# Weights loaded in two parts, a shorter routing in other steps, and high parts copied by ScalarE

## What is computed

```python
# attention: 16 heads of 8, causal
q, k, v = split(xn @ in_proj.T)
attention = softmax(q @ k.T / sqrt(8) + mask) @ v @ out_proj.T
# ffn: one shared expert and the best 2 of 7 routed ones, inner size 352
logits = xn @ wr.T + rb
probs = softmax(logits)
scores, idx = top_k(probs, 2)
scores = scores / scores.sum()
w = sum(scores * one_hot(idx, 7))
def expert(x, g, u, d): return (silu(x @ g.T) * (x @ u.T)) @ d.T
ffn = expert(xn, sg, su, sd) + sum(w[e] * expert(xn, rg[e], ru[e], rd[e]) for e in range(7))
```

## Time and profile before

| | |
|---|---|
| time, median of 3 | 493.08 us (491.39 to 498.99) |
| the profiled execution | 494.13 us |
| its span | 492.4 us |
| busy TensorE, VectorE, ScalarE, GpSimd | 442.4, 378.0, 300.3, 292.8 us |
| mean granted TensorE clock | 0.994 |

### The profile page before, as it was taken

One profiled execution on the slowest core, in us unless ns is written; L12 is line 12 of the kernel. 1 busy time (PEld: TensorE's weight loads), 2 busy tenths in 40 slices (PEclk: granted clock), 3 DMA queues, 4 the chain that ended last, 5 costly groups with the idle time before them and its releaser, 6 DMA issues.

```text
span 492.4 us, 12367 instructions
## 1 busy us (share of the span) xinstructions
PE 442.4 (90%) x3981; PEld 326.1 (66%) x3985; DVE 378.0 (77%) x915; ACT 300.3 (61%) x633; POOL 292.8 (59%) x415
## 2 busy tenths in 40 slices
PE   8988888888989999999888999989979999989995
PEld 4766555555556666666565788766867777868884
DVE  6996999899987888888774477565754888756886
ACT  2536666666767676766767666455554765655652
POOL 1446977778778888888788301643626585565200
PEclk9999999999999999999999999999989999999998
DMA  9885899889765565666364226676747577641762
GB/s 253 246 263 171 300 327 306 270 293 298 249 224 153 157 173 163 184 163 179 107 238 172 82 82 222 212 252 233 259 149 272 204 249 253 240 147 34 243 200 66
DMA packets 53215, 102.00 MB, mean 207 GB/s; under 512 B 10245, under 2 KB 28426, under 8 KB 48928
## 3 DMA queue, kind: packets, MB, share of 16 engines
q1 hardware_dynamic: 48672, 92.73, 58.5%
q0 software_dynamic: 4480, 8.47, 5.1%
HBM read 62.49 MB, written 39.46 MB: 207 GB/s over the span
## 4 chain that ended last, share of the span: by engine, by line
PE 49%; issue 6%; ACT 5%; DMA 4%; POOL 4%; DVE 3%; another core or an unknown queue 1%; SPq 0%; DVEq 0%; ACTq 0%; POOLq 0%
PE ps L801 10%; PE ps L803 9%; PE ps L802 9%; PE ps L867 4%; PE ps L928 4%; PE ps L875 3%; DMA sb_wb<-wd 3%; ACT sb_work L671 3%; POOL xs L582 2%; PE ps L1091 2%; PE ps L948 2%; POOL sb_work L606 2%; PE ps L931 2%; DVE sb_v_all L1396 1%
## 5 line engine op out<-in xcount | busy, mean ns | idle before, releaser
L671 ACT ACTIVATE sb_work<-ps 128x768 f32<-128x768 f32 x128 | 104.4, 815 | 68.8 <-PE ps L863 67.5
L1287 DVE TENSOR_REDUCE sb_blockmax<-ps 128x6 f32<-128x768 f32 x128 | 122.3, 957 | 23.8 <-PE ps L875 17.6
L627 POOL DMA_INDIRECT ys<-sb_v_all,sb_xn_all x76 | 78.6, 1035 | 93.1 <-DVE sb_v_all L1417 73.1
L606 POOL TENSOR_SCALAR_AFFINE_SELECT sb_work<-sb_work 128x512 f32<-128x512 f32 x128 | 82.5, 646 | 32.0 <-ACT sb_work L671 28.9
L802 PE MATMUL ps<-sb_ring,sb_wb 128*128 128x512 f32 (+1 forms) x231 | 83.5, 362 | 0.0
L1396 DVE TENSOR_TENSOR sb_v_all<-ps,sb_v_all 128x512 f32<-128x512 f32 (+1 forms) x93 | 57.4, 617 | 21.4 <-PE ps L803 8.0
L582 POOL DMA_INDIRECT xs<-sb_xn_all,sb_posu x64 | 62.6, 978 | 10.7 <-issue 10.7
L867 PE MATMUL ps<-sb_ring 32*128 32x256 f32 x256 | 49.2, 375 | 14.7 <-ACT sb_work L671 9.5
L751 ACT ACTIVATE sb_v_all<-ps 128x512 f32<-128x512 f32 (+1 forms) x93 | 49.6, 533 | 15.5 <-PE ps L803 12.6
L801 PE MATMUL ps<-sb_ring,sb_wb 128*128 128x512 f32 (+1 forms) x138 | 52.0, 377 | 5.4 <-issue 2.8
L867 PEld LDWEIGHTS ps<-sb_ring 32*128 32x128 f32 x256 | 25.2, 181 | 38.1 <-issue 35.3
(11 more groups left out here) (172 smaller groups left out, 1075.4 us busy)
## 6 DMA issues: line engine op xcount, KB each, us to landing
sb_wb<-wd SPq DMA_DIRECT2D x25, 1152.0 KB, 5.7
sb_ring<-qk SPq DMA_DIRECT2D x64, 256.0 KB
wd<-sb_wb SPq DMA_DIRECT2D x8, 1152.0 KB, 5.8
xs<-sb_o_all SPq DMA_DIRECT2D x19, 260.0 KB, 3.6
qk<-sb_ring SPq DMA_DIRECT2D x32, 128.0 KB
sb_work<-ys SPq DMA_DIRECT2D x16, 256.0 KB, 3.3
sb_xn_all<-xs SPq DMA_DIRECT2D x15, 260.0 KB, 3.8
sb_o_all<-w SPq DMA_DIRECT2D x8, 384.0 KB, 3.5
```

The lines of the kernel that those rows point to most:

```text
L606: pool.affine_select(out=o, in_=o, compare_op=ALU.is_ge, fill=0.0, base=0, pattern=[[0, 4], [1, 128]], channel_multiplier=-1)\
L627: pool.indirect_dma_start(out=ys_d, out_offset=bass.IndirectOffsetOnAxis(ap=row, axis=0), in_=yst[i % NYS][:, EMB * j:EMB * j + EMB], in_o ...
L671: act.activation(part.rearrange("p (k h q) -> p h k q", h=2, q=128), ps[:, 4:6, 0:HEAD].rearrange("p h (k q) -> p h k q", q=128), ACT.Exp, ...
L1287: dve.tensor_reduce(blockmax[:, a:b + 1, 0:3], ps[:, a:b + 1, 0:HEAD].rearrange("p h (k c) -> p h k c", c=128), AX.X, ALU.max).then_inc(s[ ...
```

## The change

**Weights' loads.** In `wb` and `wd` the columns are ordered by gate, up and down first and by third second, and not the other way round. `load_weights` is replaced by `load_gate_up`, which waits for the last use of gate and up of the buffer (semaphores U and G), and `load_down`, which waits for the last down product (dn) as before. Each has semaphores of its own. In SyncE's loop the order is now gate and up, tokens, down.

**Routing.** The exponentials are not divided by their sum, since the division cancels in the normalised weights of the two chosen experts; the first choice is found from b, which is zero at the maximum; the weight of the first expert is 1 / (1 + e). The two choices stand in bfloat16 and are counted by two matmuls each instead of being added first. The running sum is shifted by one place, so that the ends needn't be copied. It has 19 parts instead of 25, in the steps that N_ROUTE lists, and the counts are in steps 7 and 11.

**High parts.** The copy of L563 moves from GpSimd to ScalarE (`high_block`), behind the first of a step's two exponentials; the very first stands in the front. GpSimd's low part is made in the same steps as before.

```diff
-        N_COUNT = (11, 15)
-        N_ROUTE = 25
+        N_COUNT = (7, 11)
+        N_ROUTE = (0, 1, 2, 3, 5, 6, 7, 9, 10, 11, 13, 14, 15, 17, 18, 19, 21, 29, 33)
...
+        def block_parts(e, k):
+            to = [wb[e % 3][:, WC * h:WC * h + WC].rearrange("p (m t c) -> p m t c", t=MT, m=3)[:, :, k, :]
+                  for h in range(2)]
+            return stage[e % 2][:, WB * k:WB * k + WB].rearrange("p (m c) -> p m c", m=3), *to
...
-            def load_weights(w):
-                if w > NR + 1:
-                    return
+            def load_rows(w):
+                if 1 <= w <= NR:
+                    e = sp.value_load(etab[0:1, w - 1:w], min_val=0, max_val=ROUTED - 1)
+                    return wd[bass.ds(e * 128, 128), :].rearrange("p (h c) -> p h c", h=2)
+                return wd[ROUTED * 128:EXPERTS * 128, :].rearrange("p (h c) -> p h c", h=2)
+            def load_gate_up(w, rows):
+                if w >= 3:
+                    sp.wait_ge(s["U"], MT * (w - 3 + EARLY))
+                    sp.wait_ge(s["G"], MT * (w - 3 + EARLY))
+                to = wb[w % 3][:, :].bitcast(F32).rearrange("p (h c) -> p h c", h=2)
+                sp.dma_start(to[:, :, 0:2 * WB], rows[:, :, 0:2 * WB]).then_inc(s_wgu[w % 3], 16)
+            def load_down(w, rows):
                 if w >= 3:
                     sp.wait_ge(s["dn"], MT * (w - 3 + EARLY))
-                if 1 <= w <= NR:
-                    e = sp.value_load(etab[0:1, w - 1:w], min_val=0, max_val=ROUTED - 1)
-                    rows = wd[bass.ds(e * 128, 128), :]
-                else:
-                    rows = wd[ROUTED * 128:EXPERTS * 128, :]
-                sp.dma_start(wb[w % 3][:, :].bitcast(F32), rows).then_inc(s_wb[w % 3], 16)
+                to = wb[w % 3][:, :].bitcast(F32).rearrange("p (h c) -> p h c", h=2)
+                sp.dma_start(to[:, :, 2 * WB:WC], rows[:, :, 2 * WB:WC]).then_inc(s_wdn[w % 3], 16)
...
             for r in range(NR):
+                if r + 3 <= NR + 1:
+                    rows = load_rows(r + 3)
+                    load_gate_up(r + 3, rows)
                 load_tokens(r + 3)
-                load_weights(r + 3)
+                if r + 3 <= NR + 1:
+                    load_down(r + 3, rows)
...
-            def split_block(e, k):
-                part, low = slice(WB * k, WB * k + WB), slice(WC + WB * k, WC + WB * k + WB)
-                if k == 0:
-                    pool.wait_ge(s_wld[e % 2], LOADED[e])
-                    if e >= 3:
-                        pool.wait_ge(s_wd[e % 3], 16 * (e // 3))
-                pool.tensor_copy(wb[e % 3][:, part], stage[e % 2][:, part]).then_inc(s["wcp"], 1)
+            def low_block(e, k):
+                parts, high, low = block_parts(e, k)
                 pool.wait_ge(s["wcp"], MT * e + k + 1)
-                for c in range(0, WB, 128):
-                    a, z = part.start + c, low.start + c
-                    last = pool.tensor_tensor(wb[e % 3][:, z:z + 128], stage[e % 2][:, a:a + 128],
-                                              wb[e % 3][:, a:a + 128].bitcast(F32), ALU.subtract)
+                for m in range(3):
+                    last = pool.tensor_tensor(low[:, m, :], parts[:, m, :], high[:, m, :].bitcast(F32), ALU.subtract)
                 last.then_inc(s["wlo"], 1)
...
+            def high_block(e, k):
+                if k == 0:
+                    act.wait_ge(s_wld[e % 2], LOADED[e])
+                    if e >= 3:
+                        act.wait_ge(s_wd[e % 3], 16 * (e // 3))
+                parts, high, _ = block_parts(e, k)
+                act.activation(high, parts, ACT.Copy).then_inc(s["wcp"], 1)
...
+                        if k == 0 and n + 1 < MT * EXPERTS:
+                            high_block((n + 1) // MT, (n + 1) % MT)
...
+                if f == 13:
+                    high_block(0, 0)
...
-                    pe.wait_ge(s["selb"], 1)
+                    pe.wait_ge(s["selb"], 2)
                     pe.wait_ge(s["onesb"], 1)
                     counted = (ones_b, lt_b)[N_COUNT.index(n)]
-                    pe.matmul(out[:, 0:ROUTED * TILES], counted[:, :], selb[:, :], start=True, stop=True,
-                              skip_group_check=True).then_inc(s["cnts"], 1)
+                    for k, choice in enumerate(chosen):
+                        last = pe.matmul(out[:, 0:ROUTED * TILES], counted[:, :], choice, start=(k == 0),
+                                         stop=(k == 1), skip_group_check=True)
+                    last.then_inc(s["cnts"], 1)
...
                 if m == 0:
-                    pe.wait_ge(s_wb[loaded(i) % 3], 16 * (loaded(i) // 3 + 1))
+                    pe.wait_ge(s_wgu[loaded(i) % 3], 16 * (loaded(i) // 3 + 1))
...
+                if m == 0:
+                    pe.wait_ge(s_wdn[loaded(i) % 3], 16 * (loaded(i) // 3 + 1))
...
-                best, first, second = m_2[:, 0:n, :], m_0[:, 0:n, :], m_1[:, 0:n, :]
+                first, second = [choice.rearrange("p (e t) -> p e t", t=TILES) for choice in chosen]
                 falling = const[:, C_DEC:C_DEC + n].unsqueeze(2).to_broadcast([128, n, TILES])
                 dve.wait_ge(s["lg"], NB)
                 dve.wait_ge(s_rb, 16)
                 rt(dve.tensor_tensor(a, logit[:, 0:n, :], rb[:, 0:n].unsqueeze(2).to_broadcast([128, n, TILES]), ALU.add))
                 largest(r_s[:, 0, :], r_a)
                 yield
                 rt(dve.tensor_tensor(b, a, over(r_s[:, 0, :]), ALU.subtract))
-                yield
-                dve.memset(r_e[:, 4, 0:1], 0.0)
+                rt(dve.scalar_tensor_tensor(c, b, 0.0, falling, ALU.is_ge, ALU.mult))
+                yield
+                largest(r_s[:, 3, :], r_c)
+                dve.tensor_tensor(first, c, over(r_s[:, 3, :]), ALU.is_ge).then_inc(s["selb"], 1)
                 dve.tensor_copy(ids, const[:, C_ROW:C_ROW + TILES]).then_inc(s["id0"], 1)
                 yield
                 dve.wait_ge(s["rx"], 1)
-                summed(r_s[:, 1, :], r_a)
-                rt(dve.reciprocal(r_s[:, 2, :], r_s[:, 1, :]))
-                yield
-                rt(dve.tensor_tensor(a, a, over(r_s[:, 2, :]), ALU.mult))
-                largest(r_s[:, 0, :], r_a)
-                yield
-                rt(dve.tensor_tensor(best, a, over(r_s[:, 0, :]), ALU.is_ge))
-                rt(dve.tensor_tensor(c, best, falling, ALU.mult))
-                yield
-                largest(r_s[:, 3, :], r_c)
-                rt(dve.tensor_tensor(first, c, over(r_s[:, 3, :]), ALU.is_ge))
-                yield
+                dve.wait_ge(s["selb"], 1)
                 rt(dve.scalar_tensor_tensor(b, first, -4.0, a, ALU.mult, ALU.add))
                 largest(r_s[:, 4, :], r_b)
                 yield
-                rt(dve.tensor_tensor(best, b, over(r_s[:, 4, :]), ALU.is_ge))
-                rt(dve.tensor_tensor(c, best, falling, ALU.mult))
+                rt(dve.tensor_tensor(c, b, over(r_s[:, 4, :]), ALU.is_ge))
+                rt(dve.tensor_tensor(c, c, falling, ALU.mult))
                 yield
                 largest(r_s[:, 3, :], r_c)
-                rt(dve.tensor_tensor(second, c, over(r_s[:, 3, :]), ALU.is_ge))
-                yield
-                dve.tensor_tensor(selb[:, :].rearrange("p (e t) -> p e t", t=TILES), first, second, ALU.add)\
-                    .then_inc(s["selb"], 1)
-                rt(dve.tensor_tensor(r_s[:, 1, :], r_s[:, 0, :], r_s[:, 4, :], ALU.add))
-                rt(dve.reciprocal(r_s[:, 2, :], r_s[:, 1, :]))
-                yield
-                total, past, limit, shift, other = [r_e[:, k, 0:n] for k in (0, 4, 9, 10, 11)]
+                dve.tensor_tensor(second, c, over(r_s[:, 3, :]), ALU.is_ge).then_inc(s["selb"], 1)
+                yield
+                total, limit, shift, other = [r_e[:, k, 0:n] for k in (0, 9, 10, 11)]
+                past, ends = cum[:, 0:n, 0], cum[:, 1:n + 1, 0]
                 count2, ends2, begins2 = [r_e[:, k:k + 2, 0:n] for k in (1, 5, 7)]
                 (odd, pairs), odd_begins, pair_begins = [r_e[:, k, 0:n] for k in (1, 2)], r_e[:, 7, 0:n], r_e[:, 8, 0:n]
                 pair_ends = r_e[:, 6, 0:n]
-                flat = [rt_buf[:, k, 0:n * TILES] for k in (1, 6)]
-                rt(dve.tensor_tensor(gains, r_s[:, 0, :], r_s[:, 2, :], ALU.mult))
-                rt(dve.tensor_tensor(wt[:, :], r_s[:, 4, :], r_s[:, 2, :], ALU.mult))
+                counts, sums = rt_buf[:, 1, 0:n * TILES], rt_buf[:, 6, 1:n * TILES + 1]
+                dve.memset(rt_buf[:, 6, 0:1], 0.0)
+                rt(dve.tensor_scalar(r_s[:, 1, :], r_s[:, 4, :], 1.0, None, ALU.add))
+                rt(dve.reciprocal(gains, r_s[:, 1, :]))
+                rt(dve.tensor_tensor(wt[:, :], r_s[:, 4, :], gains, ALU.mult))
                 yield
                 dve.wait_ge(s["cnt"], 1)
-                rt(dve.tensor_tensor_scan(flat[1], flat[0], flat[0], 0.0, ALU.add, ALU.max))
```

(43 more changed lines are left out.)

## The result

| | before | after |
|---|---|---|
| time, median of 20 runs each | 494.05 us (491.39 to 501.34) | 490.56 us (486.42 to 496.46) |
| ratio after to before | | 0.9919, 95% interval 0.9897 to 0.9941 |
| profiled execution, its span | 494.13, 492.4 us | 489.56, 488.0 us |
| mean granted clock of it | 0.994 | 0.990 |

The ratio leaves out runs more than 1.5% above the fastest of their kernel. The kernel is 0.8% faster, some 4 us, where 8.6 were forecast for the profiled execution (494.13 to 485.5). Its own pair gives 4.6. Two windows of the kernel after answer to the earlier trace rows: from the first maximum of step 4 to that of step 25, and the same 212 us of the last stage. That stage is counted from the first of the two exponentials of step 63, at 269.86 us before and 268.91 after; here and in the expectations it is called the last exponential.

The account below looks back on a forecast made before the run. VectorE was taken to bound steps 4 to 24, TensorE the later steps and the last stage, with stalls at weights' loads. 494.13 - 7.0 (loads) - 1.8 (routing) + 0.2 (copies) = 485.5 us, range 479 to 492.

Parts of the forecast that it names:

- the sum of the weights' loads: Last stage (experts): loads in two parts bring weights sooner, so four stalls, a VectorE wait and slow clock go; 7.0 us.
- the two stalls marked "issue": Last stage, first matmuls of tiles behind a weights' load: TensorE idle 1.05 and 1.74 us, forecast to go.
- the 0.5 us of a wait behind the first: Half tile after the 1.05 us stall: of a 0.86 us wait for VectorE, 0.5 was counted as gained.
- the 1.7 us of slow clock behind the second: After the 1.74 us stall: TensorE's granted clock averages 0.83 over 10 us, 1.7 us of work lost, counted as gained.
- The hold of SyncE: Before the 1.74 us stall: load issued at 352.35, next instruction at 357.67, read as SyncE held for 5.3 us.
- the two stalls that a load did end: Last stage, first matmuls of tiles: stalls of 1.44 and 0.58 us; their going alone was the lower bound, 2.0 us.
- The routing: First 25 steps: steps 4 to 24 take 78.2 us instead of 83.24, 5.0 less; 1.8 us gained net of moved operations.
- the emptied steps: Steps 4, 8, 12, 16, 20 and 24, left without routing: 3.5 us each, not 3.00, because of TensorE's side matmuls.
- rival C: VectorE alone sets the first 25 steps and moved operations hide: 478.1 us, 481.8 likelier, cases 477 to 483; chance 0.20.
- the four terms, 0.3, 1.0, 0.8 and 1.1: Time in us the routing gives back in steps 1, 2, 29 and 33, where operations are added or moved.
- rival D: Copies on ScalarE lie on the exponentials' path and delay the next scores; fully exposed 14.2 us, 499.7; chance 0.08.
- B: Loads stay a bound, as SyncE's holds delay early parts too: only 2.0 of 7.0 comes, 490.5, cases 488 to 493; chance 0.17.

## Why the prediction was wrong

**The step that failed is the sum of the weights' loads, 7.0 us, and in it the two stalls marked "issue", 1.05 and 1.74 us.** They were taken for late loads, and with them went the 0.5 us of a wait behind the first and the 1.7 us of slow clock behind the second: 5.0 of the 7.0 us. The trace of before shows that no weights' load was under way in either; both loads had moved their bytes 3 us before TensorE fell idle. The hold of SyncE, which was the reason to count them, was a wait for a scatter. What is left is 2.0 us for the two stalls that a load did end, and measured, the part is worth 2.7 us of 480 on the third chip (interval 1.0 to 4.4) and 1.2 of 494 on the first, with an interval that reaches from a gain of 3 to a loss of 0.5.

The mechanism held for those two: in every profile with divided loads no tile waits for a load. In the seven with whole loads TensorE waits for one, 1.7 to 3.6 us in the four on the later chips, 2.0, 1.8 and 0.2 us in the three on the first. More on the rest of the sum:
- What ended the "issue" stalls is not known. In four of the first chip's six profiles, with whole, divided and no loads, TensorE has a wait of over 0.4 us at four places some 20 us apart, and on that chip VectorE and ScalarE are late for "issue" and unknown queues too; the later chips have next to none of this. The wait for VectorE's low part is 7.5 and 8.1 us with divided loads there and 4.9 to 5.9 with whole ones, but 5.3 with none, so that the loads' gain went into it isn't shown.
- The slow clock (1.7 us) came behind a stall at a tile's start in two of the seven profiles with whole loads, before and the routing alone, and in none of the ten others in this stage. As a mean over executions it is nearer 0.5 us than 1.7.
- I set one profile's stage, 222.54 us, as the base; 216 to 217.5 is what the next four profiles on that chip show.
- The 0.5 us of the VectorE wait behind the first stall didn't go: that kind grew.

**The routing was right in its sum, in part by luck.** At a full clock steps 4 to 24 gained 6.0, forecast 5.0: the emptied steps took 3.4 each and not 3.5, steps 22 and 23 took 3.17 and not 3.43, and the other thirteen 50.6 together, forecast 50.3. Why the emptied steps stay at 3.4, above the 3.0 of VectorE alone (rival C), isn't shown. Given back were 3.0 in the profile of after and 3.1 on the third chip, forecast 3.2. But of the four terms, 0.3, 1.0, 0.8 and 1.1, the profile of after shows 0.4, 1.1, 0.3 and 0.2; the rest lies in steps that the sum left out, 0.4 in step 25 for one. Net 1.8 forecast, 2.9 on the third chip. A term was missing that went the other way: in seven of the nine profiles with this routing the clock falls at step 21, and in four at step 5. The profile of after has both and 78.71 us, the routing alone on the third chip neither and 77.25, so it gained 4.5 and not 6.0.

**The copies** cost nothing, as forecast (ratio 0.9993 alone, and 0.32 us or more to spare in every step but the first); the 0.2 for step 0 can't be seen, and rival D is out. But they weren't needed to shorten the steps.

**The rivals.** B came out at 490.5, which is the measured time, yet for a wrong reason: no load stayed a bound, and SyncE wasn't held. Its low end, 2.0 us for what DMA alone had ended, was the nearest term, because it left out just what the trace didn't give to a DMA. The Trainium skill (DMA: Bandwidth & Descriptors, Bandwidth) says to batch transfers to 1 MiB or more; the 768 and 384 KB parts here gave a ratio of 0.9944 against the whole of 1152 KB, so the earlier start counted for more. Its fixed cost of about 2 us, which the prediction cites, is given for DMAs issued by GpSimd; these are issued by SyncE, and no run here measures it.

## What to carry to other kernels

Count a stall for a transfer only where the trace says that the transfer ended it, and where it says "issue", look at whether the queue moved anything in just that idle time: 0.84 and 0.87 of the DMA engines' time in the two real stalls here, 0.18 and 0.04 in the two others. A gap between two DMA issues is no hold of the engine before the waits of the second have been read. Before a stage's stalls are added up, profile the kernel twice, and compare the mean granted clock of two sets of runs before a difference of 0.5% is put down to the code. Work moved off a full engine is worth what the next engine leaves, 3.4 and not 3.0 us a step here.

## What was not expected of the hardware

- **The chips differ by 3% in this kernel.** Before took 493.84 us on one and 478.11, 479.88 and 480.27 on three others. Most of it is in the last stage: the loads alone, profiled on the first and the third chip at a mean clock of 0.997 both times, took 216.4 and 205.7 us there, 129.4 and 126.8 from step 25 to that stage, and 83.3 in steps 4 to 24 on both. In before on the first chip VectorE waited 11.6 us in the last stage for "issue" or an unknown queue and ScalarE 8.6; in eleven profiles on the others there is one such wait, of 0.6 us. What it is that differs isn't shown.
- **The clock falls behind short waits too, and not each time.** Ahead of the kernel's last 5 us, 17 profiles have 23 stretches at 0.50: 17 of 3.4 us, five of 6.8 and one of 10.2, which cost 1.7, 3.4 and 5.1 us of clock. Seven of the nine profiles with the change's routing steps have one at 121 to 127 us, at step 21, behind two waits of TensorE of 0.62 and 0.67 us; step 21 then takes 4.5 to 4.8 us instead of 3.7. The two others have the same two waits and a full clock.
- **The time of a run goes with its clock.** Of the 29 runs of before on the third chip the nine with a mean granted clock of 0.995 or more average 477.3 us, those below 0.99 480.7, without the three longest. That is 3.4 us, where the whole change is worth 5.6 on that chip.
